# Twelve page scatters a turn straight from the normalised tiles, unit experts from a table, places in three operations

## The reference

```python
x = x + xattn(layernorm(x), ctx_768)          # 16 heads of 8, 64 keys a batch
y = layernorm(x)                              # (4096, 128)
shared = silu(y @ sg_w.T) * (y @ su_w.T) @ sd_w.T
scores = sigmoid(y @ gate_w.T) + gate_bias    # 64 experts in 8 groups, 4 groups kept
topk_w, topk_i = top_k(scores * mask, 6); topk_w /= topk_w.sum()
h = silu(y @ eg_w[e].T) * (y @ eu_w[e].T)     # for each chosen expert e
x = x + shared + sum(topk_w * (h @ ed_w[e].T))
```

## Time and profile before

| | before |
|---|---|
| runs | 802.83, 804.34, 805.97 us, median 804.34 |
| span of the profiled execution | 792.4 us |
| what lies around the span, taken as median minus span | 11.9 us |
| busy TensorE / VectorE / ScalarE / GpSimd | 503.3 / 456.1 / 352.3 / 389.3 us |
| first stage, to VectorE's last place | 0 to 400.5 us |
| quads | 400.5 to 748.5 us |
| gathers left over | 748.5 to 792.4 us |

### The profile page before, as it was taken

One profiled execution on the slowest core, in us unless ns is written; L12 is line 12 of the kernel. 1 busy time (PEld: TensorE's weight loads), 2 busy tenths in 40 slices (PEclk: granted clock), 3 DMA queues, 4 the chain that ended last, 5 costly groups with the idle time before them and its releaser, 6 DMA issues.

```text
span 792.4 us, 12061 instructions
## 1 busy us (share of the span) xinstructions
PE 503.3 (64%) x3204; PEld 420.8 (53%) x3204; DVE 456.1 (58%) x2264; ACT 352.3 (44%) x962; POOL 389.3 (49%) x425
## 2 busy tenths in 40 slices
PE   3767555766555574632359956788688889777700
PEld 2445334444334343311359856778688789777700
DVE  6587556667555576656233624576776756346532
ACT  3564433344443343322215934466666766246400
POOL 2006445654455655556650055454554545555574
PEclk9885555555555555555568976899988876897555
DMA  7532123322123332223425533455455555654421
GB/s 195 194 113 94 62 100 107 104 100 98 47 80 107 107 100 98 95 78 129 124 81 134 148 94 95 106 138 151 126 145 137 151 137 146 160 153 107 113 70 47
DMA packets 98708, 90.60 MB, mean 114 GB/s; under 512 B 10576, under 2 KB 85456, under 8 KB 98640
## 3 DMA queue, kind: packets, MB, share of 16 engines
q1 hardware_dynamic: 85232, 64.26, 27.5%
q0 software_dynamic: 12288, 25.29, 11.3%
q10 hardware_dynamic: 1120, 0.28, 0.2%
HBM read 41.32 MB, written 48.46 MB: 113 GB/s over the span
## 4 chain that ended last, share of the span: by engine, by line
PE 30%; another core or an unknown queue 17%; issue 16%; ACT 14%; POOL 11%; DVE 9%; ACTq 2%; DMA 0%; POOLq 0%; DVEq 0%
PE bank_s L1155 14%; POOL pages L447 6%; PE bank_o L1155 4%; PE bank_q L1155 3%; PE bank_s L1151 2%; ACT d_now L511 2%; ACT p_t L533 2%; ACT pxt L511 2%; POOL empty L492 2%; ACT gu_now L511 2%; ACT k_exp L521 1%; ACT s_act L672 1%; POOL p_t L492 1%; PE bank_o L1151 1%
## 5 line engine op out<-in xcount | busy, mean ns | idle before, releaser
L1155 PE MATMUL bank_s<-pxt,gu_now 128*128 128x64 f32 x768 | 116.5, 316 | 51.6 <-ACT pxt L511 31.3
L492 POOL DMA_INDIRECT p_t<-results,place_i x96 | 91.1, 949 | 110.6 <-ACT s_act L672 72.8
L1155 PEld LDWEIGHTS bank_s<-pxt,gu_now 128*128 128x128 f32 x768 | 111.4, 231 | 58.1 <-ACT pxt L511 36.4
L492 POOL DMA_INDIRECT empty<-results,place_i x96 | 91.1, 949 | 77.2 <-issue 35.1
L1111 DVE TENSOR_TENSOR h_t<-bank_s,s_act 64x256 f32<-64x256 f32 x128 | 54.7, 427 | 113.9 <-ACT s_act L672 95.4
L447 POOL DMA_INDIRECT pages<-payload,place_i x96 | 93.0, 968 | 37.9 <-issue 27.0
L447 POOL DMA_INDIRECT pages<-payload_b,place_i x96 | 92.8, 967 | 35.8 <-issue 26.7
L437 POOL TENSOR_TENSOR rstd<-ve,minus_half 128x4 f32<-128x4 f32 (+1 forms) x21 | 18.6, 885 | 132.6 <-DVE ve L927 130.0
L672 ACT ACTIVATE s_act<-bank_s 64x512 f32<-64x512 f32 x64 | 37.8, 590 | 79.5 <-remote 36.0
L533 ACT ACTIVATE p_t<-bank_s 128x512 f32<-128x512 f32 x64 | 36.2, 598 | 67.9 <-issue 27.9
L1255 PE MATMUL bank_o<-bias_h,row_h 96*128 96x256 bf16 x16 | 6.1, 381 | 72.2 <-ACT o_t L511 70.3
(11 more groups left out here) (169 smaller groups left out, 1164.1 us busy)
## 6 DMA issues: line engine op xcount, KB each, us to landing
pg<-pages SPq DMA_DIRECT2D x64, 258.0 KB
results<-y_s SPq DMA_DIRECT2D x64, 256.0 KB
pages<-empty SPq DMA_DIRECT2D x21, 774.0 KB
w_gu<-in_expert_gu SPq DMA_DIRECT2D x16, 256.0 KB
w_d<-in_expert_d SPq DMA_DIRECT2D x31, 128.0 KB
out_x<-xb SPq DMA_DIRECT2D x16, 128.0 KB
xb<-in_x SPq DMA_DIRECT2D x3, 512.0 KB, 8.0
pages<-payload,place_i POOLq DMA_INDIRECT x96
```

Of the source, the lines that this page charges most:

```text
L492: pool.indirect_dma_start(out=ys[n % YS_SLOTS][:, k, :], out_offset=None, in_=results[0:landed * QUAD * P, :], in_offset=bass.IndirectOffs ...
L1155: return pe.matmul(dst, w, v, start=True, stop=True)
```

## The change

- **Scatters straight from `xn2`.** `payload`, `fill_payload` and the expert column are gone; page rows are 128 wide. `xn2` has six slots in place of two, and a slot is free when the twelve scatters of the batch six before have landed.
- **Twelve a turn.** GpSimd starts all twelve scatters of batch b-3 in turn b, and the power for body b+1 behind them.
- **Places in three operations a batch.** `is_expert` (a comparison over 2 tiles x 6 choices x 64 experts, bf16, placed inside `find_rows`), `picked` (a product with `row`) and a sum over the 64 that writes integers. Both tiles are ready at one time.
- **Unit experts from a table.** `next_page` is kept for all batches. After quad 0's products VectorE counts, for every unit, how many entries lie at or under it (`count_units`, nine operations); TensorE packs the experts of each half quad into codes (`pack_codes`, at quad 2), VectorE copies them (`keep_codes`, at quad 3). `pack_experts` is gone from the quads, and SyncE's page loads no longer wait for it.
- **Separate DRAM buffers** for the pages and results of batches 0 to 13 and of 14 and 15.

```diff
-            def scatter(n, t, first, after):
-                wait_payload(n, t)
-                for k in range(first, after):
-                    pool.indirect_dma_start(out=pages[:, :], out_offset=bass.IndirectOffsetOnAxis(
-                        ap=place_i[:, TPB * n + t, k:k + 1], axis=0), in_=payload[n % 2][:, t, k, :],
-                        in_offset=None).then_inc(scattered[n % 2][t], 16)
+            def scatter(n, t, k):
+                if t == 0 and k == 0:
+                    pool.wait_ge(place_ready, n + 1)
+                    pool.wait_ge(xn2_ready, TPB * (n + 1))
+                    pool.wait_ge(prefilled, 16 * fills_before(n))
+                pool.indirect_dma_start(out=(new_pages if n >= SPLIT else old_pages)[:, :], out_offset=bass.IndirectOffsetOnAxis(
+                    ap=place_i[:, TPB * n + t, k:k + 1], axis=0), in_=xn2[n % XN2_SLOTS][:, t, :],
+                    in_offset=None).then_inc(scattered[n % XN2_SLOTS], 16)
+            def sent_by(b):
+                return max(0, SENT_A_TURN * (b - 2) - HELD_BACK)
+            for b in range(FIRST_BODY - 1, BODIES_END):
+                scatters(sent_by(b - 1), sent_by(b))
                 if any_norm(b + 1):
                     inverse_deviations(b + 1)
-                if on(n):
-                    if ahead < TOPK:
-                        scatter(n, 0, ahead, TOPK)
-                    if ahead < 2 * TOPK:
-                        scatter(n, 1, max(0, ahead - TOPK), TOPK)
...
+                chained("is_expert", dve.tensor_tensor(
+                    is_expert[:, :, :, :], iota_h[:, :].unsqueeze(1).unsqueeze(1).to_broadcast([P, TPB, TOPK, E]),
+                    experts(expert_h[:, :, :]), ALU.is_equal))
...
-                for k in range(TOPK):
-                    place_step(n, ("pick", t, k), dve.scalar_tensor_tensor(
-                        out=picked[:, k, :], in0=iota_e[:, :], scalar=expert_f[:, t, k:k + 1], in1=row[:, t, :],
-                        op0=ALU.is_equal, op1=ALU.mult, accum_out=place[:, t, k:k + 1]))
+                place_step(n, "pick", dve.tensor_tensor(picked[:, :, :, :], is_expert[:, :, :, :],
+                                                        row[:, :, :].unsqueeze(2).to_broadcast([P, TPB, TOPK, E]), ALU.mult))
...
+                    dve.tensor_reduce(place_i[:, TPB * n:TPB * (n + 1), :], picked[:, :, :, :], AX.X, ALU.add).then_inc(place_ready, 1)
...
-            def pack_experts(q):
...
+            def count_units():
+                for c in range(UNIT_TILES + 1):
+                    batches, tile = (slice(0, SPLIT), c) if c < UNIT_TILES else (slice(SPLIT, B), 0)
+                    size = batches.stop - batches.start
...
+                    dve.scalar_tensor_tensor(out=at_or_under[:, 0:size, :], in0=next_page[:, batches, :], scalar=unit[:, tile:tile + 1],
+                                             in1=ones_e[:, :].unsqueeze(1).to_broadcast([P, size, E]), op0=ALU.is_le, op1=ALU.mult,
+                                             accum_out=opened_by[:, c:c + 1]).then_inc(counted, 1)
...
```

More of the change, by code:

```diff
@@ L79, with build @@
 UPFRONT = 5
-MADE = 8
-POWER_AFTER = {}
-def build(nc, x, ctx_cols, wq, bq, wk, bk, wv, bv, wo, bo, gate_cols, gate_bias, expert_gu, expert_d, shared_gu, shared_d, out, pages, results):
+MADE = 9
+XN2_SLOTS = 6
+A_BATCH = TPB * TOPK
+SENT_A_TURN = 12
+HELD_BACK = 0
+def build(nc, x, ctx_cols, wq, bq, wk, bk, wv, bv, wo, bo, gate_cols, gate_bias, expert_gu, expert_d, shared_gu, shared_d, out, old_pages, new_pages, old_results, new_results):
     with ExitStack() as ctx:
@@ L163, in build @@
         o_t = sb("o_t", [P, TOK])
[L165 removed]
+        xn2 = [sb(f"xn2_{i}", [P, TPB, D]) for i in range(XN2_SLOTS)]
         sig = sb("sig", [P, TPB, E])
@@ L453, in body @@
-            def body(b):
-                n = b - 3
-                ahead = POWER_AFTER.get(n, TOPK)
-                if on(n):
-                    scatter(n, 0, 0, min(ahead, TOPK))
-                    if ahead > TOPK:
-                        scatter(n, 1, 0, ahead - TOPK)
+            def scatter(n, t, k):
[6 more added lines that the diff above has]
+                    in_offset=None).then_inc(scattered[n % XN2_SLOTS], 16)
@@ L460, in body, with scatters @@
+            def sent_by(b):
+                return max(0, SENT_A_TURN * (b - 2) - HELD_BACK)
+            def scatters(first, after):
+                for i in range(first, after):
+                    n, place = divmod(i, A_BATCH)
+                    scatter(n, place // TOPK, place % TOPK)
+            for b in range(FIRST_BODY - 1, BODIES_END):
+                scatters(sent_by(b - 1), sent_by(b))
                 if any_norm(b + 1):
                     inverse_deviations(b + 1)
-                if on(n):
-                    if ahead < TOPK:
-                        scatter(n, 0, ahead, TOPK)
-                    if ahead < 2 * TOPK:
-                        scatter(n, 1, max(0, ahead - TOPK), TOPK)
@@ L468, in _ @@
-            for b in range(FIRST_BODY - 1, BODIES_END):
-                body(b)
+            scatters(sent_by(BODIES_END - 1), B * A_BATCH)
             def beat(step):
@@ L1104, in quad @@
             def quad(q):
-                if q + 2 < NQ and held(q + 2) is None:
-                    pack_experts(q + 2)
                 dve.wait_ge(act_ready, q + 1)
```

231 lines of the change are left out of this document (131 added, 100 removed).

## The result

The changed kernel took 825.99 us (median of 4, 817.99 to 830.62), the kernel before 803.59 us (802.59 to 805.97): ratio 1.0251, interval 1.0182 to 1.0319. The sign was forecast; 813 us and the upper end 822 were not enough. The profiled execution of the changed kernel was its longest, 830.62 us with a span of 828.9 (as were those of e1, e2 and e12); in e5's trace (span 825.8) the middle bodies have the same length, 25.46 us against 25.49, so I read the first one.

What follows compares the result with a forecast made beforehand. No engine bounds the kernel, a chain does, and the power would wait for twelve scatters: first-stage bodies +15.5, power 17 to quads -3, packs -3.5, sum +9 us; span 801.4 plus 11.9 around it gives 813 us, range 796 to 822.

Steps and rivals of the forecast that it cites:

- the upper end 822: Top of the forecast range: the three place operations at their upper bound and the table's count in the open.
- The loop: Middle bodies: power, `nmr` and `filled_to`, places, twelve scatters make 23.8 us a body against 23.49, +2.8 over bodies 4 to 12.
- Body 3, bodies 13 to 15, body 16: Remaining first-stage bodies, set by scatters ahead of the power: +6.0, +3.3 and +3.4 us.
- The three operations: VectorE's new places: comparison 0.89, product 0.89, sum 0.97 us, +1.25 us to the places, bounds +0.8 and +1.8.
- Scatters of 512-byte rows: GpSimd's scatters: rows of 512 instead of 516 bytes take 949 against 968 ns, twelve 14.7 us instead of 14.9.
- The fills at nothing: ScalarE: removing two copies a body of 0.84 us each, and the last fill, gains nothing.
- Power 17 to the quads: End of the first stage: fewer picks remove small VectorE waits, -3 us, bounds 0 and -15.5.
- the faster rival: VectorE's short waits from power 16 to the first quads go: 800 us, 796 if quads gain too; chance 0.27.
- the -3.5 of the packs: Quads: removing the two `pack_experts` operations, 0.38 us each quad, gains 3.5 us.
- The table: Quad 0: VectorE's count of units, 5.4 us, is hidden in idle time and adds 0.
- The likeliest: First stage: the power waits for its twelve scatters, 813 us, own range 808.5 to 822; chance 0.55.
- the rival at +0.8: Edge of the 0.55 case: places only +0.8 us later, loop 23.35, only bodies 3 and 13 to 16 add, 807 us.

Runs made afterwards that it cites:

- e1: Changed kernel with the last six of a batch's twelve scatters issued behind the next power: 768.51 us, ratio 0.9753 to the kernel before.
- e2: Changed kernel with all twelve scatters of a batch issued behind the next power: 783.89 us, ratio 0.9884 to the kernel before.
- e12: Changed kernel in its own order, GpSimd waiting after the eighth scatter for ScalarE's copy of the next ranks: 828.41 us, ratio 1.0466 to the kernel before.
- e5: Changed kernel, unchanged, measured again on another chip: 827.6 us, ratio 1.035 to the kernel before.
- e4: Changed kernel with each scatter replaced by a GpSimd power of 4 elements a partition, no rows written to the pages: 740.3 us in one run.
- e3: Kernel before with only the scatter order changed, all twelve of a batch ahead of the next power: 811.37 us, ratio 1.0307.
- e7: Changed kernel with six scatters behind the power, each sending rows of 64 partitions instead of 128: 774.67 us in one run.
- e8: Changed kernel with six scatters behind the power, the table of units counted three times: 791.44 us, ratio 0.9883 to the kernel before.
- e10: Kernel before with GpSimd waiting for ScalarE's o_t after the eighth scatter behind a power: 760.85 us, ratio 0.9496.
- e6: Changed kernel with six scatters behind the power, GpSimd waiting for ScalarE's o_t after a turn's eighth scatter: 743.29 us, ratio 0.9314 to the kernel before.

## Why the prediction was wrong

**The loop: the step that failed.** "Power 1.04, `nmr` and `filled_to` 0.2" took it that ScalarE's ranks are there when the power ends. They were not: 3.32 us from the power to `filled_to`, not 1.24. e4 and e12 show the difference to be the hold (1.12 and 1.16 us without it). I had read the earlier trace rows, where `filled_to` waited 0.33 us for the ranks, and moved the scatters past the power without asking who else runs while they are issued. The other terms were close, on the dear side: 6.96 us from `filled_to` to the places for 7.26 (+1.10 for +1.25 by e3), scatters with their gaps 15.25 for 15.3, so without the hold the loop is 23.3, not 23.8. So a turn came out at 25.5 and bodies 4 to 12 at +18.0 for +2.8.

**Body 3, bodies 13 to 15, body 16:** +6.6 for +6.0, +5.6 for +3.3, +3.1 for +3.4. Bodies 15 and 16 have no such wait for the ranks, and there the loop was right (23.08 us for 23.45, 22.32 for 22.6). In e5's trace body 3 is 24.5 us, +4.5, and power 4 stands at 77.25, where it was forecast.

**The three operations** took 952, 902 and 944 ns in the mean, against estimates of 0.89, 0.89 and 0.97 us. The comparison ran at single rate, as the Trainium skill ("VectorE: DVE Perf Modes", "What auto-detection actually checks") has it for an operand with step 0. The formula used with it stands in the same page's section "The TRN2 errata — SBUF-src ops pay a fixed extra latency per instruction", for fp32; its 957 ns agree with the trace's 952.

**Scatters of 512-byte rows** took 969 ns, not less than the 968 of the earlier trace rows. e7 shows how little was to be had: half the rows save 0.07 us of 0.96.

**The fills at nothing** may have been wrong. e1 puts everything but the order at -2.5%, though the longer way to tile 0's places alone should have made it slower. How much of it is the fills and how much the places of both tiles together, no run separates; what e1's rows show is that the sigmoid gets through ahead of the hold.

**Power 17 to the quads.** I gave back 3 us within bounds of 0 and 15.5; it was 15.1, the upper bound. The small waits did go, as the faster rival had it. Why is not shown: this stretch is 16.6 us in the changed kernel and 16.7 to 17.3 in nine other runs built on it, but 33.1 us in e7, with the same instructions on VectorE and the small waits back. So it was luck as far as the working goes, and fewer instructions are not enough to explain it. But "GpSimd's last scatters end later too, so nobody waits" failed: ScalarE waited, 20.65 us, most of it for a product that TensorE had done. From the last place to the end of the quads it is 362.70 us for 348.00, and the -3.5 of the packs is not to be seen. From the second `s_act` to TensorE's last product it is even 338.3 us for 331.9, and this part is not explained: TensorE's granted clock from the last place to the end of the quads is 0.80 for 0.82, but no run varied it.

**The table** was hidden, as forecast, though by a stall (e8).

**The rivals.** The likeliest had the right mechanism: the power follows the twelfth scatter, `nmr` waits for it. The faster one, weighed at 0.27, had its 15 us where it said, and they were taken away by what none of the cases held.

**The upper end.** 822 was to hold "three operations at their upper bound, table in the open". By the terms of the sum that is 14 bodies x (1.8 - 1.25) = 7.7 and 5.4 on top of 813.3, 826.4 us. Such an upper end would have lain over the measured 825.99 only by luck, for neither happened (+1.10 us, and a hidden table). In the rival at +0.8 body 3 would add 5.6 by the same working, not 4.5.

```profile
123.42 0.42 DVE L927 TENSOR_TENSOR xb<-bank_o,xb 128x256 f32<-128x256 f32 x1 [3.70 <-remote]
...
244.62 0.42 DVE L904 TENSOR_TENSOR xb<-bank_o,xb 128x256 f32<-128x256 f32 x1 [5.96 <-remote]
```

Nor is the hold total or always to the run's end: in body 10 of the changed kernel VectorE's `xb` ran at 250.12, in the middle of the run of scatters (244.11 to 259.05), 0.03 us after TensorE's end; e3's `o_t` was let go at 241.06, with six scatters still to come; e1's sigmoid and e10's exponentials run during the scatters.

Not found are what delays the signals, whether TensorE's work itself is late or its signal alone (the ends of its instructions are modelled), and what decides which signal is caught. Whether the issuing or the traffic does it is not separated either: e4 takes both away, e7 halves only the rows, and in the changed kernel's body 9 the last packet of the run ended at 234.43, 1.3 us before `xn_t` was let go. One rival falls: this was no wait for instructions to be loaded. In the window 223.00 to 236.50, which spans the wait of 11.24 us, only one queue moved anything. The window's DMA queues:

```profile
DMA packets 291, 0.59 MB, mean 44 GB/s; under 512 B 147, under 2 KB 147, under 8 KB 291
...
q0 software_dynamic: 291, 0.59, 13.0%
```

The Trainium skill has instructions fetched by a DMA queue of the sequencer's own ("Runtime: NRT & Kernel Launch", "Instruction fetch mechanics"); no packet of such a queue moved in this window, while the window 210 to 222 lists two.

## What to carry to other kernels

When instructions that start indirect transfers are to be gathered into one run, look for waits of other engines that end with no releaser shown, and compare their ends with the end of the run; here one of them cost 2.1 us in each turn and another lasted 20.65 us. See also whose signal they waited for: that engine, and not the one that stands, may be the one held. A pause in such a run, placed where an engine on the path is due, can be worth more than every operation saved: e10's one wait gave 5%, all parts of the change but the order 2.5%. And before a stage is said to be covered, see what happens to the cover.

## What the runs showed of the hardware

- While GpSimd issued indirect transfers, TensorE's semaphores were raised late: up to 8.9 us behind the recorded end in the middle bodies of the changed kernel, 0.09 us at most in e4 without such transfers. Signals of the other engines came within 0.01 us.
- Waits of ScalarE on these signals ended 1.3 us after the last transfer in e1, 1.7 in e2, 2.2 in the changed kernel and in e7, 1.44 and 1.6 us after a pause began in e6 and e12, 2.3 and 2.8 for the second `s_act` in e5 and in the changed kernel; in e3 one ended 1.0 us after a transfer with more to come. With computing operations of the same number in their place (e4) the wait went from 11.24 to 1.61 us.
- The instruction for an indirect transfer of 128 rows took 0.96 us, for 64 rows 0.89, and the next one started 0.30 us behind it; twelve took 14.96 us up to the next operation.
- Twelve powers of 4 elements a partition took 11.74 us back to back, 0.98 each.
